# Rotary turning of k taken out of the scan loops: GpSimd turns it between them, through DRAM

## The reference

```python
x = x + mamba(layernorm(x), ...)          # conv, silu, selective scan with 16 states, gate, out projection
x = x + cross_attention(layernorm(x), ctx, ctx, positions, mask, Wq, Wk, Wv, Wo)
x = x + experts(layernorm(x), A, B, Wq, keys)   # top 16 of 64 gates, rank 8 each
# in the attention: 32 q heads on 8 k/v heads of width 128
# q = q * cos + rotate_half(q) * sin ; k likewise, with cos and sin looked up by each token's position
```

## Time and profile before

| | us |
|---|---|
| three executions | 2399.07, 2400.57, 2403.79 |
| median | 2400.57 |
| profiled execution, first to last instruction (span) | 2396.3 |

### The profile page before, as it was taken

The page is one execution under the profiler, slowest core; times in us unless marked ns, Lnnn a source line. Parts: engine busy times, 40 slices in busy tenths (PEclk is TensorE's granted clock), DMA queues, the critical chain, the costliest instruction groups (busy, mean ns, idle before and its releaser), DMA issues.

```text
span 2396.3 us, 27137 instructions
## 1 busy us (share of the span) xinstructions
PE 2107.1 (88%) x8244; PEld 1194.4 (50%) x8248; DVE 1786.4 (75%) x1801; ACT 1059.8 (44%) x2613; POOL 588.9 (25%) x405
## 2 busy tenths in 40 slices
PE   6877888989999979989999979989999987799987
PEld 2332453445555534445555534445555533577763
DVE  3499994389999975289999985279999984355533
ACT  2544441465565522365665522365655521243330
POOL 0099981001111120001111110001111120566530
PEclk9888999899999989899999989889999999799888
DMA  1468893148888771238888871238888772122210
GB/s 62 166 152 198 213 213 121 54 133 187 181 177 187 166 173 53 72 123 179 176 189 179 181 172 60 72 106 172 176 196 175 171 173 82 65 90 97 88 44 18
DMA packets 110074, 328.98 MB, mean 137 GB/s; under 512 B 12945, under 2 KB 13073, under 8 KB 107569
## 3 DMA queue, kind: packets, MB, share of 16 engines
q0 software_dynamic: 35328, 127.94, 28.7%
q1 hardware_dynamic: 68912, 189.58, 26.3%
q10 hardware_dynamic: 5760, 10.49, 1.2%
HBM read 183.00 MB, written 14.94 MB: 83 GB/s over the span
## 4 chain that ended last, share of the span: by engine, by line
DVE 40%; PE 31%; issue 18%; DMA 5%; ACT 3%; DVEq 1%; POOL 1%; SPq 1%; POOLq 0%; ACTq 0%; PEldq 0%
DVE hs L1130 13%; PE acc L1443 5%; DVE hs L1137 5%; DVE hs L1300 5%; PE pq L1488 4%; DMA xc<-hs 3%; DVE hs L1121 3%; DVE qr L1167 2%; PE pq L1732 2%; PE pq L1496 2%; PE pq L1526 2%; PE acc L1655 2%; PE pk L1732 2%; PE acc L1565 2%; DVE sc L1187 1%
## 5 line engine op out<-in xcount | busy, mean ns | idle before, releaser
L706 POOL DMA_DIRECT2D xc<-hs x192 | 165.8, 866 | 1301.6 <-DVE hs L1137 1263.9
L1130 DVE TENSOR_TENSOR_SCAN hs<-dA,hs 128x1024 f32<-128x1024 f32 x192 | 428.9, 2276 | 0.0
L888 ACT ACTIVATE dA<-dt,aneg 128x504 f32<-128x504 f32 x384 | 253.5, 707 | 250.9 <-DVE hs L1130 250.7
L1496 PE MATMUL pq<-qT,wa 128*128 128x512 f32 x768 | 354.8, 616 | 9.2 <-DVE sc L1187 9.2
L1576 PE MATMUL acc<-wb,oT 128*128 128x512 f32 x768 | 351.7, 602 | 3.6 <-ACT oT L876 3.6
L1137 DVE TENSOR_TENSOR hs<-hs,bc 128x1024 f32<-128x1024 f32 x256 | 307.9, 1205 | 2.2
L853 ACT ACTIVATE pr<-sc,mx 128x64 f32<-128x64 f32 x512 | 170.8, 335 | 247.4 <-DVE mx L1193 247.4
L1443 PE MATMUL acc<-xnT,wa 128*128 128x512 f32 x512 | 232.2, 607 | 11.5 <-PE acc L1443 4.4
L1496 PEld LDWEIGHTS pq<-qT,wa 128*128 128x128 f32 x768 | 146.9, 197 | 183.8 <-issue 173.7
L1121 DVE TENSOR_TENSOR hs<-u,bc 128x1024 f32<-128x1024 f32 x192 | 226.3, 1219 | 8.2 <-ACT xc L976 5.9
L1526 PE MATMUL pq<-kT,qp 128*128 128x64 f32 x1024 | 190.9, 289 | 41.2 <-DVE kT L1146 16.3
(11 more groups left out here) (200 smaller groups left out, 3312.7 us busy)
## 6 DMA issues: line engine op xcount, KB each, us to landing
xc<-hs POOLq DMA_DIRECT2D x240, 512.0 KB, 6.9
bc<-bc_rows SPq DMA_DIRECT2D x64, 512.0 KB, 7.5
wa<-in_wq SPq DMA_DIRECT2D x64, 512.0 KB, 10.2
wb<-in_wo SPq DMA_DIRECT2D x64, 512.0 KB, 5.8
wa<-in_wx SPq DMA_DIRECT2D x16, 512.0 KB, 4.2
wa<-in_wz SPq DMA_DIRECT2D x16, 512.0 KB, 4.9
wb<-in_ow SPq DMA_DIRECT2D x16, 512.0 KB, 7.2
k<-k_rows SPq DMA_DIRECT2D x32, 256.0 KB, 11.1
```

The source lines that it names most:

```text
L888: ins = S.activation(to[:, :, 1:SEQ], dt[:, s, :].rearrange("p (b t) -> p b t", t=SEQ)[:, :, 1:SEQ], ACT.Exp, scale=aneg[:, s, bass.ds(jj ...
L1130: V.tensor_tensor_scan(out=hs[:, c, :], data0=dA[:, c % 2, :], data1=hs[:, c, :], initial=0.0, op0=ALU.mult, op1=ALU.add).then_inc(scd.sem, 1)
L1496: ins = M.matmul(pq[:, h, :], wa4(p)[:, k, h * P:(h + 1) * P], qT[:, k, :], start=(k == 0), stop=(k == KE - 1))
```

## The change

- `turned` and `tscr` are new DRAM tensors: turned k of blocks 0 to 2 (eight groups each) and the tables (cos and negated sin) of all four blocks.
- At the start all positions are loaded and clipped at once, and GpSimd issues the 16 gathers of all blocks, into buffers that are not yet in use. In steps 0 to 3 of iteration 0's loop two more early units each transpose one block's tables, and ScalarE stores them. The load of block 0's residual `xr` moves behind these.
- Between the loops SyncE loads `cosT` and `sinT` of the next attention ahead of the out-projection weights. It no longer loads raw k of blocks 0 to 2 there.
- In iterations 0 to 2 GpSimd, behind its ln2 `rstd`, turns block i's k in four rounds of two groups (`turn_k`): load raw and swapped, two multiplications, subtraction, store to `turned`. The buffers are `qp` and `qr`; each round waits for the store of the one before.
- At the end of iterations 0 to 2 SyncE waits for the fourth store and loads the first turned group into `kT` and, swapped, `k2T`. In the loops it loads the next group into these same buffers once the last scores that read them are done.
- In iterations 1 to 3 VectorE's `rope_k` and ScalarE's `turn_k` are gone. Block 3's k is still turned by VectorE in iteration 4.

```diff
         def early_units(n):
             ks = [("k", n // 4, (2 * n + d) % KVH) for d in range(2)]
+            if n < NBLK:
+                return ks + [("table", n, 0), ("table", n, 1)]
...
# SyncE
-                            if p == 0:
-                                eng.wait_ge(krdy.sem, krdy.upto(blk, 0) + jj)
+                            if p == 0 and mamba:
+                                eng.wait_ge(sd.sem, sd.upto(blk, 1) + jj * 2)
                                 hold(eng)
-                                load_k(blk, jj + 1)
+                                load_turned_k(blk, jj + 1)
...
                     for n in range(W_KE):
                         load_wb(i, at_b + n, a["bw"][n])
+                if nxt:
+                    eng.wait_ge(s_kst, i * (8 * KVH) + 8 * KVH)
+                    hold(eng)
+                    load_turned_k(i, 0)
                 if attn:
                     eng.wait_ge(outr.sem, outr.upto(blk, 0))
                     eng.dma_start(out[blk], xn).then_inc(s_out, 16)
...
# GpSimd
+            eng.wait_ge(s_pid, 1)
+            for b in range(NBLK):
+                for t in range(TT):
+                    eng.indirect_dma_start(
+                        out=tab(b, t), out_offset=None, in_=a["rotary"],
...
+                def turn_k(m):
+                    raw, swp = qp[:, :, :].rearrange("p b w -> p (b w)").rearrange("p (g t) -> p g t", t=T), qr
+                    if m:
+                        eng.wait_ge(s_kst, i * (8 * KVH) + 16 * m)
+                        hold(eng)
+                    G.dma_start(raw, kscr[i, 2 * m:2 * m + 2].rearrange("g p t -> p g t")).then_inc(s_kraw, 16)
+                    for h in range(2):
+                        G.dma_start(swp[h * 64:(h + 1) * 64, :, :],
+                                    kscr[i, 2 * m:2 * m + 2, (1 - h) * 64:(2 - h) * 64, :].rearrange(
+                                        "g p t -> p g t")).then_inc(s_kraw, 16)
+                    two = [P, 2, T]
+                    eng.wait_ge(s_kraw, i * (24 * KVH) + 48 * (m + 1))
+                    hold(eng)
+                    G.tensor_tensor(raw, raw, cosT[:, :].unsqueeze(1).to_broadcast(two), ALU.mult).then_inc(kc1.sem, 1)
+                    G.tensor_tensor(swp[:, :, :], swp[:, :, :], sinT[:, :].unsqueeze(1).to_broadcast(two),
+                                    ALU.mult).then_inc(kc2.sem, 1)
...
+                    G.tensor_tensor(raw, raw, swp[:, :, :], ALU.subtract).then_inc(kcd.sem, 1)
...
+                    G.dma_start(turned[i, 2 * m:2 * m + 2].rearrange("g p t -> p g t"), raw).then_inc(s_kst, 16)
...
# ScalarE
-                    if attn and mamba and p == 1 and not tail:
-                        turn_k(jj + 1)
...
# VectorE
-                        if p == 0:
+                        if not mamba and p == 0:
                             rope_k(jj + 1)
```

More of the change, by code:

```diff
@@ L589, in one @@
                 if mamba:
-                    eng.wait_ge(pid.sem, pid.upto(i, -1))
-                    hold(eng)
-                    eng.dma_start(posi[:, :], a["pos"][i]).then_inc(s_pos, 16)
+                    if attn:
+                        eng.wait_ge(q1r.sem, q1r.upto(blk, PAIRS - 1))
+                        hold(eng)
+                        eng.wait_ge(q2r.sem, q2r.upto(blk, PAIRS - 1))
+                        hold(eng)
+                    else:
+                        for n in range(2):
+                            eng.wait_ge(s_est[n], 16 * (first_unit[NS] // 2))
+                    load_tables(i)
                     if not attn:
@@ L602, in one @@
                 if mamba:
[L604 to L610, removed]
+                    if not nxt:
+                        load_raw_k(i, 0)
                     if nxt:
@@ new lines, in one @@
+                if nxt:
+                    if attn:
+                        eng.wait_ge(sd.sem, sd.upto(i - 1, PAIRS - 1))
+                    else:
+                        for n in range(2):
+                            eng.wait_ge(s_est[n], 16 * (first_unit[NS] // 2))
+                        eng.wait_ge(scd.sem, scd.upto(0, NS * NCH - 1))
+                    eng.wait_ge(s_cs, i * 32 + 32)
+                    hold(eng)
+                    for m in range(KVH // 2):
+                        turn_k(m)
@@ L981, in one, with read_unit @@
                         S.activation(silu_z(s), acc[:, s % 4, :], ACT.Silu).then_inc(szr.sem, 1)
-                def read_unit(at, what):
+                def read_unit(at, what, b, g):
+                    scale = float(D) ** -0.5 if what == "k" else -1.0 if what == "table" and g == 1 else 1.0
                     eng.wait_ge(s_eun, at + 1)
@@ L1628, in one @@
                     eng.wait_ge(outr.sem, outr.upto(blk, -1))
-                    eng.wait_ge(s_tab, blk * (16 * TT) + 16 * TT)
-                    hold(eng)
-                    for c in range(2):
-                        for t in range(TT):
-                            ins = M.transpose(pq[:, c, t * P:(t + 1) * P], tab[:, t, c * D:(c + 1) * D],
-                                              ident[:, :])
-                    ins.then_inc(rot.sem, 1)
                 if mamba:
@@ L1675, in early_unit @@
                     ctx_t = early_ctx[b % 2]
+                    if what == "table":
+                        eng.wait_ge(s_tab, 16 * TT * NBLK)
+                        for t in range(TT):
+                            ins = M.transpose(acc[:, 2 + at % 2, t * P:(t + 1) * P], tab(b, t)[:, g * D:(g + 1) * D],
+                                              ident[:, :])
+                        ins.then_inc(s_eun, 1)
+                        return
                     eng.wait_ge(s_ectx[b % 2], 16 * (b // 2 + 1))
```

142 lines of the change are left out of this document (81 added, 61 removed).

## The result

The change makes the kernel slower. Four executions of it took 2430.79 to 2442.30 us, median 2435.35, and before took 2399.82 (median of four): 1.0147 times as long, 95% interval 1.0122 to 1.0172, 35.5 us. In a second series it took 2434.08, 1.0156 times as long (1.0132 to 1.0181). The profiled execution has a span of 2429.1 us against 2396.3, so 32.8 us are to be found in the trace. Forecast was +12 us, in a range that reached to 2460.

A forecast was written before the change was run, and what follows sets the result against it. VectorE was taken to bound the loops, with TensorE close behind, and TensorE the stretches between. Terms -29 - 8 + 42 + 2 + 6 = +13 (unrounded +12) on the 2400.6 us median gave 2413 us, range 2390 to 2460.

The forecast's parts named there:

- Direction and rival waits: Whole kernel: slower (chance 0.61), because SyncE's wait for the fourth store between loops delays the first wq load.
- A round of 19.7 us: Between loops, one GpSimd turning round: loads 7.0, operations 7.9, store 4.5, semaphores 0.3; four rounds take 79 us.
- The DMA rule: GpSimd DMAs between loops: 2.0 us plus bytes over 436 GB/s, loads 4.4, store 3.2; round 15.8, sum -11.
- The SBUF rule: Between loops: VectorE locks GpSimd out only with two SBUF inputs or 2-port mode; operations near 2.35 us, sum about +3.
- First stretch +42: Between block 0's loop and the next: first q projection waits for wq, 40 us late, plus 2 us restart.
- The 2 us for a slow restart: First stretch: after idling TensorE restarts slowly, four matmuls in 3.78 us instead of 1.88, charged at 2 us.
- Second and third, +2 and +6: Later stretches between loops: turning delays wq and so the first q projection, by 2 us and 6 us.
- -4 each for `ow`: Second and third stretch: out-projection weights load earlier, removing TensorE's wait and slow restart; 8 us less together (0 to 13).
- Loops -29: Three loops: k turns leave VectorE, each pair of steps saves about 1.4 us, 21 pairs give 29 us less (11 to 42).
- TensorE's circle: Loops: tightest path through TensorE and VectorE, 30.7 + 12.5 + about 0.1 = 43.3 us a pair, longer than VectorE's 42.69.
- The third rival: Loops: TensorE takes over at once, a pair keeps 44.2 us, only 11 us come back; 2432 us, chance 0.12.
- Block 0 "nothing, up to 5": Block 0: sixteen gathers and eight table units fit beside other work; taken at nothing, up to 5 us.

The follow-up runs named there:

- the two kernels put together first: Change plus turned-k wait behind wq and wo loads, out-projection weights ahead of tables, wv early, rows after fourth sum; one or two buffer sets: 2403.84 and 2410.32 us.

## Why the prediction was right or wrong

The forecast had the direction and the main cause right, and 35.5 us were measured where it had 12. Three of its steps failed: the bound of a pair of steps in the loops, the clock behind the wait for wq in the second stretch, and block 0's loop, put at nothing. A fourth error, the length of a round in the first stretch, went the other way and hid a part of them.

- **Direction and rival waits: right.** Slower, by SyncE's hold of wq, was what was forecast, and where.
- **A round of 19.7 us: 18.2 to 18.5** in the first stretch, where four took 73.5 us instead of 79. Loads 6.6 (7.0), operations 7.2 (7.9), store 3.8 (4.5), and 0.6 us between the last operation and the store's issue (0.3 for all semaphores). In the second and third stretch one store each landed late (6.8 and 7.3 us instead of 3.2) and four rounds took 80. In the other execution of the change the four of the first stretch took 76.1.
- **The DMA rule** (Trainium skill, *DMA: Bandwidth & Descriptors*, "Anatomy of one DMA"): the store's landing, 3.2 us in the median, is its estimate to the tenth. The loads took 6.6 us where the estimate, made as for a single DMA of 1 MB, gives 4.4; in the trace they are three DMAs, whose issues alone take 1.95 us one behind the other. With rounds of 15.8 us the estimate's sum of -11 is further off than the forecast's.
- **The SBUF rule** (Trainium skill, *SBUF — State Buffer*, "Who interferes with whom"): GpSimd ran at 2.34 to 2.37 beside the convolution, so the trace agrees, and 2.63 was too slow.
- **First stretch +42: +35.5 and +40.1** in two executions, block 0's later out projection in it. In the first the q projection starts 35.3 us later after the last scan, and not 40: the rounds were 5.5 us quicker and wq landed 0.5 sooner, but GpSimd started 1.3 later, behind the out projection, whose weights stand behind the table loads (1.7 us here, 3.0 in the other execution, where the q projection waits 36.8). The 2 us for a slow restart were in the q projection (1.9), and the dt projection gave 1.5 of them back.
- **Second and third, +2 and +6, with -4 each for `ow`: +2.1 and +3.8**, against -2 and +2. The `ow` part was right (the out projection runs 4.0 to 5.4 us earlier from there on). The wq wait was right in the second, where the projection starts at 132.1 us after the last scan instead of 134.2, 2 us earlier as forecast; in the third it starts 3.3 us later (132.4 instead of 129.1) and not 2. What failed is that a slow restart was charged in the first stretch alone. In the second, 5.4 us of idling brought 2.8 us up to the end of the dt projection and 1.4 in the next q projection (10.00 instead of 8.61), which is the whole of the 4 us missed. In the third, 7.4 us of idling slowed the q projection by 2.2, but the dt projection took 2.6 less; with 0.9 in the next q projection 0.5 are left.
- **Loops -29: -22.2.** The step that failed is "longer than 42.69", the choice of TensorE's circle as the bound. VectorE did follow its own work where it could (42.68), and the wait that kept it from that, 0.94 us a pair, was in no step: the landing of the fourth chunk's sum. I had read the sums' landing only as a price for other DMAs, and not asked which wait the k turn covered. That the forecast's pair (43.3) is only 0.4 short of the measured 43.7 is luck: another mechanism makes it. The turned k was loaded in time, as costed: TensorE waits for it nowhere in the loops. The third rival's total (2432 us) came close by luck too. Its pair of 44.2 and its 11 us of gain are further from 43.7 and 22.2 than the forecast's, and no run shows TensorE as the bound.
- **Block 0 "nothing, up to 5": about 4.** The table units and the gathers were weighed, the moved x[0] load wasn't: 2 to 4 us are its part, the rest, about 2 us, is open, and the table units' stores are not ruled out for it. The order in SyncE's queue cost the out projection besides. I had asked of the queue only what stands behind the wait for turned k, not what stands behind the moved table loads.

The sum of the misses: loops +7, later stretches +6, block 0's loop +4, the first stretch -6, the start and the part behind the last loop +10 in this execution: about +20, the difference between 32.8 and 12. In the other execution, with a span 30.9 us longer than before, it is +7, +6, +5, -2 and +2. So of the two last pieces it is not known how much belongs to the change.

## What to carry to other kernels

When a wait goes into a queue of loads, list everything that stands behind it up to the next point where the queue would have waited anyway, and put the wait behind what others need first: moving one wait behind three loads gave back 39 us, 29 to 35 of them in the stretches that it held up. When work is taken off a busy engine, look for the wait that it covered: a landing which ended just in time is the next bound, and it is found by setting each buffer's landing against its next use. A combination of good parts has to be measured: a second buffer set gained 17 us in one stretch and lost 21 in two others, between the two kernels put together first.

## What the hardware showed besides

- **Small VectorE operations can be shut out for as long as GpSimd keeps working**: 7.6 us instead of 0.74 for four operations of 128x64 beside three GpSimd operations back to back, in four stretches of two kernels. In the forecast I had only asked what VectorE does to GpSimd.
- **A summing DMA of 512 KB lands in 5.1 to 14.4 us in the same loop.** With the row and wq loads held back until the fourth chunk's had landed, 10.2 was the longest there.
- **TensorE got 1.2 GHz for about 4 us after 5.4 idle us** (granted 0.50, rows above), and the q projection took 2.5 us more. Look at what follows before charging it: where the clock had fallen in the next matmuls anyway (third stretch), 2.6 us of it came back there.
